# The stretch between the two layers of a graph network kernel: another order of SyncE's transfers, edge ends in pairs, count checks inside the second product, and conversions taken from GpSimd

## The reference

```python
h = jnp.maximum(_layernorm(x), 0.0)                       # layer 0
ea = edge_attr @ W_edge.T + b_edge
msg = relu(h[src] + ea)
aggr = segment_sum(msg, dst, num_segments=N_NODES)
u = relu(((1.0 + eps) * h + aggr) @ W1.T + b1)
x = x + u @ W2.T + b2                                     # "second product" = u @ W2.T

h = jnp.maximum(_layernorm(x), 0.0)                       # layer 1
m = relu(h[src]) + EPS
ex = exp(m - segment_max(m, dst)[dst])
msg = segment_sum(ex / segment_sum(ex, dst)[dst] * m, dst)
x = x + (h + msg) @ W + b
```

## Time and profile before

| | us |
|---|---|
| time, median of 3 runs | 2461.71 |
| lowest, highest | 2456.18, 2465.78 |
| the profiled execution's own time | 2460.79 |
| its span (what the trace covers) | 2459.0 |
| layer 0 and its end (trace, to about) | 2026 |
| two products, layer norm, `table16` and its transfers (to about) | 2120 |
| layer 1 (from the third block on) | 339 |

### The profile page before, as it was taken

The page is one execution under the profiler, slowest core; times in us unless marked ns, Lnnn a source line. Parts: engine busy times, 40 slices in busy tenths (PEclk is TensorE's granted clock), DMA queues, the critical chain, the costliest instruction groups (busy, mean ns, idle before and its releaser), DMA issues.

```text
span 2459.0 us, 54222 instructions
## 1 busy us (share of the span) xinstructions
PE 1809.7 (74%) x11221; PEld 1497.2 (61%) x11222; DVE 1908.5 (78%) x4568; ACT 760.4 (31%) x1320; POOL 1767.9 (72%) x1801
## 2 busy tenths in 40 slices
PE   3677776767766776766766767776767767699999
PEld 2466665655555565655655556655655655588887
DVE  9999997878778887878787878777887878354454
ACT  5001121222233333344444444444544555000000
POOL 4777777777777777777777777777777762477774
PEclk9899888888888888888888888887888896899999
DMA  5234344444444444444444455454554533877774
GB/s 162 48 83 105 95 108 106 108 105 113 115 107 127 122 118 120 122 130 125 129 126 127 133 129 136 135 139 126 149 134 128 145 111 133 292 270 259 263 273 151
DMA packets 172680, 344.69 MB, mean 140 GB/s; under 512 B 72897, under 2 KB 126971, under 8 KB 158286
## 3 DMA queue, kind: packets, MB, share of 16 engines
q1 hardware_dynamic: 33586, 153.14, 21.2%
q0 software_dynamic: 60864, 99.55, 17.9%
q10 hardware_dynamic: 77990, 89.82, 10.7%
HBM read 247.65 MB, written 94.68 MB: 139 GB/s over the span
## 4 chain that ended last, share of the span: by engine, by line
POOL 59%; issue 19%; PE 15%; DVE 2%; DMA 2%; SPq 2%; ACT 1%; POOLq 0%; ACTq 0%; DVEq 0%
POOL rows_buf L585 59%; PE ps L849 11%; PE ps L859 2%; DMA rows_buf<-table,index 1%; PE ps L680 1%; SPq L531 1%; SPq L545 1%; ACT features_buf L932 0%; DVE zone L1364 0%; PE ps L826 0%; PE ps L872 0%; PE ps L772 0%; DVE ps L1327 0%; SPq L537 0%; PE ps L670 0%
## 5 line engine op out<-in xcount | busy, mean ns | idle before, releaser
L585 POOL DMA_INDIRECT rows_buf<-table,index x1539 | 1511.6, 982 | 496.5 <-issue 493.2
L772 PE MATMUL ps<-zone,planes 128*128 128x400 f16 x2352 | 620.5, 379 | 555.9 <-DVE zone L1364 467.1
L1364 DVE TENSOR_SCALAR zone<-iota_c,planes 128x400 f16<-128x400 int16 x2352 | 678.1, 341 | 60.9 <-issue 50.9
L990 ACT ACTIVATE features_buf<-ps 128x800 f16<-128x800 f32 x392 | 327.8, 836 | 1240.2 <-PE ps L772 1233.7
L772 PEld LDWEIGHTS ps<-zone,planes 128*128 128x128 f16 x2352 | 251.3, 107 | 733.6 <-issue 675.7
L670 PEld LDWEIGHTS ps<-wet,zone 128*128 128x128 f32 x3136 | 551.0, 250 | 35.3 <-issue 30.5
L670 PE MATMUL ps<-wet,zone 128*128 128x96 f32 x3136 | 535.7, 330 | 0.0
L657 PE MATMUL ps<-onehot,features_buf 128*96 128x128 f32 x3120 | 428.4, 283 | 0.0
L657 PEld LDWEIGHTS ps<-onehot,features_buf 128*96 128x96 f32 x3120 | 395.1, 174 | 12.0 <-issue 1.3
L1327 DVE TENSOR_TENSOR ps<-ps,rows_buf 128x768 f32<-128x768 f32 x171 | 164.6, 963 | 256.1 <-DMA rows_buf<-table,index 235.5
L1125 DVE TENSOR_TENSOR planes<-ps,planes 128x1536 f16<-128x1536 f32 x196 | 341.3, 1741 | 0.0
(11 more groups left out here) (186 smaller groups left out, 811.0 us busy)
## 6 DMA issues: line engine op xcount, KB each, us to landing
counts<-features_buf ACTq DMA_DIRECT2D x392, 200.0 KB
zone<-edge_t SPq DMA_DIRECT2D x98, 768.0 KB
single<-table SPq DMA_DIRECT2D x3072, 0.4 KB
rows_buf<-counts SPq DMA_DIRECT2D x24, 1600.0 KB, 6.8
rows_buf<-table,index POOLq DMA_INDIRECT x1539
planes<-counts SPq DMA_DIRECT2D x12, 1600.0 KB
weighted<-planes SPq DMA_DIRECT2D x5, 840.0 KB
final<-residual ACTq DMA_DIRECT2D x48, 48.0 KB
```

Of the source, the lines that this page charges most:

```text
L585: nc.gpsimd.indirect_dma_start(out=into[:, t, :], out_offset=None, in_=table, in_offset=bass.IndirectOffsetOnAxis(ap=at[:, t:t + 1], axis= ...
L772: nc.tensor.matmul(count_ps[:, bass.ds(banks[k], WC)], row_hot[:, u % 2, g * GS + k, :], pair_hot[:, g * GS + k, :], start=False, stop=Fal ...
L990: nc.scalar.activation(count_out[:, k], bank, ACT.Copy, accum_out=row_sum[:, bass.ds(p, 1)]).then_inc(moved, 1)
L1364: last = nc.vector.tensor_scalar(pair_hot[:, k, :], iota_c[:, :], step_pair[:, bass.ds(i * (IS * SC) + (u * SC + k), 1)], None, ALU.is_equal)
```

## The change

Five things change, all between the layers.

1. **Order on SP.** The waits and stores are put in another order (the rows below). The counts of block 1 still wait for `node_out`; those of block 2 come after the fifth unit's own rows. A unit's store of the four parts (`weighted_store`) stands among the stores of own rows (`own_store`). The two loads of `own` stand before the last `weighted_store`.
2. **Edge ends in pairs.** `edge_src` and `edge_dst` are one input `edge_ends[2, ...]`, and a fetched block's sources and destinations come in one transfer of twice as many rows: 13 transfers instead of 26.
3. **Count checks.** The three small PE instructions stand after the first of the ten groups of the second product, the matmul for `block_start` after the fourth, and DVE copies `block_start` in the loop after the second unit's moments.
4. **No GpSimd conversions.** The high part of exp(h) is made by DVE for units 0, 1 and 3, and by ACT for units 2 and 4. GpSimd only gathers.
5. **HBM tensors.** `hidden` and `weighted` are gone; own rows go to `table0`, the four parts to `table1` seen as float16 (same shapes and sizes). ACT reads its copy of the flag inside the loop instead of ahead of it.

```diff
@@ sp @@
+                def own_store(u):
                     sp.wait_ge(features, NU + u + 1)
                     for part in (slice(0, EVEN), slice(EVEN, NP)):
-                        sp.dma_start(hidden.rearrange("(p j) d -> p j d", j=NJ)[part, units[u], :],
+                        sp.dma_start(own_rows.rearrange("(p j) d -> p j d", j=NJ)[part, units[u], :],
                                      hs[part, units[u], :]).then_inc(own_out, 16)
...
+                block_load(0)
+                sp.wait_ge(starts_ready, 1)
+                for g, start in enumerate(load(sp, block_start, DB, GB, [E] * GB)):
+                    n = FETCH[g]
+                    sp.dma_start(fetch_ends[:, :, FETCH_AT[g]:FETCH_AT[g] + n],
+                                 edge_ends[:, bass.ds(start, P * n)].rearrange("e (p k) -> p e k", k=n)
+                                 ).then_inc(fetch_in, 16)
+                sp.wait_ge(node_out, NG)
+                block_load(1)
...
+                for u in range(NU - 2):
+                    own_store(u)
+                weighted_store(0)
+                weighted_store(1)
+                own_store(NU - 2)
+                weighted_store(2)
+                own_store(NU - 1)
+                block_load(2)
+                weighted_store(3)
                 sp.wait_ge(own_out, 2 * NU * 16)
                 sp.wait_ge(step_done, SC + NSTEP)
                 for b in range(2):
-                    sp.dma_start(own[:, b, :], hidden[b * P:(b + 1) * P, :]).then_inc(residual_in[b], 16)
+                    sp.dma_start(own[:, b, :], own_rows[b * P:(b + 1) * P, :]).then_inc(residual_in[b], 16)
+                weighted_store(4)
@@ pe @@
+            def count_checks(g):
+                if g == 0:
+                    pe.wait_ge(bad_ready, 3)
+                    nc.tensor.transpose(ps[0:1, 6, 0:P], bad[:, 2:3], ident[:, :])
...
+                if g == 3:
+                    pe.wait_ge(edges_moved, 1)
+                    nc.tensor.matmul(ps[0:1, 5, 0:NB], block_edges[:, :], upper[0:NB, 0:NB], start=True, stop=True
+                                     ).then_inc(starts_ps, 1)
...
                     last.then_inc(node_ps, 1)
+                    if layer == 0:
+                        count_checks(g)
@@ act @@
                 exp_of(3)
+                exp_high_of(2)
                 product_high(2)
                 feature(1, NU - 1)
                 exp_of(4)
+                exp_high_of(4)
@@ dve @@
                 moments_of(1, u)
+                if u == 1:
+                    dve.wait_ge(starts_ps, 1)
+                    nc.vector.tensor_copy(block_start[:, :], ps[0:1, 5, 0:NB]).then_inc(starts_ready, 1)
```

More of the change, by code:

```diff
@@ L80 @@
 NE = 4
+HIGH_ON_ACT = (2, 4)
 NW2 = 2
@@ L1627 @@
     dst_tiles = tiles(dst, QT * P, NPAD)
[L1628 to L1630 removed]
+    ends = np.zeros((2, E + EPAD), np.int32)
+    ends[1] = NPAD
+    ends[0, :E] = np.asarray(src)
+    ends[1, :E] = np.asarray(dst)
     arrays = {
```

90 lines of the change are left out of this document (38 added, 52 removed).

## The result

The changed kernel takes **2429.1 us** (median, 2425.8 to 2431.2) where the kernel before takes 2460.3 (2456.2 to 2465.8) beside it: a ratio of 0.987 (95% interval 0.985 to 0.989). The forecast of 2448.9 us and its range from 2445 to 2455 are both missed; the gain is 31 us and not 12.8. The profiled execution has a span of 2424.0 us against 2459.0 before, 35.0 us less.

A forecast was written before the change was run, and what follows sets the result against it. It took SP's queue between the layers to delay layer 1, which runs at PE's pace. Gathers gain 10.0 us (8.7 + 0.9 + 0.4), plus 2.8 spare: 12.8 off the median 2461.7 gives 2448.9 us, range 2445 to 2455.

The forecast's parts named there:

- 59% of it is GpSimd's gathers of layer 0, which the change leaves alone: Layer 0: its gathers are 59% of the chain and keep their time; only what lies behind them is at stake.
- I cost the whole conversion item at nothing: Between the layers: moving GpSimd's five conversions gains 0 us, being covered by transfers; 3 us cost if the cover were gone.
- The prediction's own test: Layer 0: the forecast is wrong if its 2026 us move by more than 1 us.
- Edge ends ahead of `node_out`: SP's queue: 13 pairs from 2058.6 at 0.52 us each take 6.8 us, ending at 2065.4, ahead of 2066.8.
- The slower rival: SP's queue: a paired transfer takes longer than two did; slower from 1.6 us each, 2468.4 us at 2.1; chance 0.03.
- The hole closes: SP's queue: legs of 16.2 and 28.5 us join without the 8.7 us hole, saving 0.9 us start-up; gathers 9.6 us earlier.
- Conversions on DVE and ACT: Between the layers: DVE gets three, ACT two, about 1.0 us each, against GpSimd's 3042 ns for each of five.
- Count checks: Second product: ten matmul rows run in PE's 2.13 us wait; gain 0.4 us on `node_out`, ends 0 and 1.3.
- `own` ahead of the last parts: SP's queue: `own` lands 10.0 + 3.0 = 13.0 us earlier, at 2106.5; PE's 20.0 us wait shrinks to 7 to 9.
- the rival in which `own` comes no earlier than the parts: Start of layer 1: `own` lands no earlier than the parts, PE and gathers both gain 10.0 us: 2451.7 us; chance 0.10.
- What is late next: Layer 1, second fetched block: gathers start 10.0 us earlier with 2.8 us spare, allowing a gain of 12.8 us.
- the rival of the gathers behind a block's counts: Layer 1: gathers queue behind 1600 KB of counts, up to 4.6 us late; gain 8.2, 2453.5 us; chance 0.12.

The follow-up runs named there:

- e4: Kernel before, masked, with SyncE's new order and moved count checks alone, two transfers for each block's edge ends: 2455.5 us, ratio 0.996.
- c0: Kernel before, with the wait values that ACT and PE load from memory masked to 16 bits: 2462.1 us, ratio 1.002.
- the control: Changed kernel with masked wait values and no other edit, run on the same chip as the early loads of `final`: 2428.7 us, ratio 0.986.
- e1: Kernel before, masked, with own rows in `table0` and the four parts in `table1`, no other edit: 2457.4 us, ratio 0.999.
- e2: Kernel before, masked, with the five conversions moved from GpSimd to DVE (three) and ACT (two), no other edit: 2442.8 us, ratio 0.993.
- e3: Kernel before, masked, with the edge ends in 13 transfers of pairs in the old place, no other edit: 2451.6 us, ratio 0.997.
- f5: Changed kernel, masked, with ACT issuing the loads of `final` for the first four blocks ahead of its wait for own rows: 2434.4 us, ratio 0.988.

## Why the prediction was wrong, by its own steps

**"59% of it is GpSimd's gathers of layer 0, which the change leaves alone."** This is the step that failed, together with **"I cost the whole conversion item at nothing"**. The price was looked for where the conversions stand, and there it is nothing: the seam takes 52.7 us instead of 53.1 without them, and 42.5 instead of 41.8 with them, both within its spread. But GpSimd's instructions between the layers set the price of all its gathers, and 1539 of them in a chain turn 11 ns into 17 us. It is nearly the whole distance of 20 us between forecast and result. Why the gathers take that price is open (see above); that it comes with the conversions is shown from both sides. The prediction's own test, that layer 0's 2026 us must not move by more than 1 us, is what caught it. The seam alone would have given some 12 us, and 2449 us. The profiled pair of executions flatters the change by some 4 us more, which are TensorE's clock (an estimate: 3.0 us in the first product and 0.9 behind it, by the numbers under the count checks).

**Edge ends ahead of `node_out`: right.** 0.52 us for a pair was chosen between 0.52 and 1.04, and 0.53 measured (6.92 / 13). They ended at 2042.1, 1.0 us before SP went past `node_out` (1.4 forecast). `e4` shows the other end: 1.0 us for two, 4.0 us late. The slower rival needed 1.6 us for a pair. The rule quoted with it (the Trainium skill, "DMA: Bandwidth & Descriptors", section "Why a DMA increments its semaphore by 16 and not by 1"), sixteen DMA engines where 128 is outermost, agrees with the trace. SP's queue shows these packets for the 13 transfers, from 2035.2 to 2043.5:

```profile
q1 hardware_dynamic: 3536, 0.25, 31.9%
```

That is 13 x 272. The rows of ends are 13 x 256, and the other 208, of 4 bytes each, are 16 for a transfer.

**The hole closes: right but for 0.9 us.** The two legs, 16.2 and 28.5 us, sum to 44.7, and from the counts of block 1 (2043.15) to the first gather (2087.89) it takes 44.7 us. The hole of 8.7 us is gone to a tenth. The 0.9 us taken for one start of an empty queue less did not appear.

**Conversions on DVE and ACT: right in the seam.** DVE's took less than the 1.0 us assumed, ACT's as much (line, busy us, mean ns):

```profile
L1042 ACT ACTIVATE planes<-zone 125x960 f16<-125x960 f32 x2 | 2.0, 996 | 0.0
L1492 DVE TENSOR_SCALAR planes<-zone 125x960 f16<-125x960 f32 x3 | 2.0, 654 | 0.0
```

**Count checks: right in kind, 0.4 us forecast and some 0.9 found.** The table above doesn't show this, because the clock moves its rows. Ahead of the second product PE stood for 2.7 us behind the first (2.1 of waiting, then the three small instructions) in all five kernels with the old place of the checks, and 1.3 us in all fifteen with the new one. In these 1.3 us it waits for the first product's results on DVE, so the product begins 1.4 us sooner and not the whole 2.7:

```profile
2023.06 1.33 PE L700 MATMUL ps<-w2s,rows_buf 96*125 96x96 f32 x10 [1.30 <-DVE rows_buf L1452]
```

Half a microsecond of the 1.4 comes back inside the product. From the end of the first product to the last addition, `c0` and `e4`, at the same granted clock:

```profile
2044.37:2068.36 23.99, 21.43 (x108) 20.79 (x107) 20.19 (x108) 9.91 (x28) 0.00 (x0) 0.57 0.19 70
2042.92:2066.01 23.09, 21.11 (x107) 20.22 (x107) 20.18 (x109) 9.90 (x28) 0.00 (x0) 0.57 0.28 80
```

It is 0.9 us less with the checks moved, inside the prediction's ends of 0 and 1.3. The clock takes the rest of the 4.2 us: it lies between two levels here (0.50 is 1.2 GHz, 1.00 is 2.4). It was 0.61 on average from 2028 to 2036 in the kernel before, in the first product, and 1.00 in the same place of the changed one; the whole first product took 16.2 and 13.2 us. From its end to the last addition it was 0.59 and 0.85, in 23.2 and 21.4 us, of which 0.9 are the checks. The control had 0.79 and 14.5 us:

```profile
2028.00:2036.00 8.00, 8.00 (x26) 5.26 (x25) 6.06 (x12) 2.54 (x5) 0.00 (x0) 0.61 0.08 28
```

```profile
2009.00:2017.00 8.00, 7.85 (x31) 5.35 (x32) 6.36 (x14) 3.43 (x6) 0.00 (x0) 0.79 0.08 28
```

The first of these rows is of the kernel before, the second of the control. This isn't the change's doing: `e1`, `e2` and `e3`, which have neither the new order nor the moved checks, ran their first product in 13.1 us at 1.00.

**`own` ahead of the last parts: right mechanism, some 1.3 us too much.** PE's turn came 11.3 us earlier behind `node_out` where 12.6 (13.0 without the checks' 0.4) were forecast: 0.9 is the start-up that didn't appear, 0.2 the 2.8 us by which PE gained on the gathers instead of 3.0, and the last 0.2 is not accounted for. PE gained more than the gathers did (11.3 and 8.6 us), so the rival in which `own` comes no earlier than the parts fell. PE's wait is 10.5 us, not 7 to 9, because PE's work ahead of it ended 31.2 us behind `node_out` (2084.90 - 10.54 - 2043.12) instead of 33.1. Whether `final` or `own` lands last changes nothing, as `f5` shows.

**What is late next: right.** The gathers start 3.0 us behind PE's turn, where it was 0.2, and layer 1 takes 339.1 us as before. The only wait of PE behind its first turn is one of 2.1 us, which the kernel before has too:

```profile
PE ps L881 <- DVE soft L1570: 2.1, 1, 2.1
```

So the rival of the gathers behind a block's counts fell. The rule that spoke against it (the Trainium skill, "DMA: Bandwidth & Descriptors", section "Queues, rings and completion order": queues take turns packet by packet) fits the trace, which shows no wait there; no run shows the turns themselves.

## What to carry to other kernels

What else runs on an engine that issues one instruction 1500 times in a chain can change the price of that instruction: before costing an edit on that engine at nothing because it is off the path, multiply a change of one per cent in that instruction by its count, and keep that in the range. Put small transfers where the queue is empty: the same 13 took 6.9 us there and 15.6 behind 5.6 MB, 9.4 of them in two at which SP was stopped, so read such a group transfer by transfer and not by its mean. When two small loads are issued together into a full queue, advancing one alone gave nothing here. Before reading a stretch of a few microseconds between two traces, see whether both had the same granted clock in it.

## What was not expected of the hardware

- A gather of GpSimd takes 955 or 944 ns over a whole execution, and three or five tensor_scalars executed between the layers, behind the last gather of layer 0 (57 to 2036 us later in the kernel before), decide it, even of 128x1 and 0.2 us each. One doesn't, five ahead of the first gather don't, five that aren't run don't.
- GpSimd's fourth instruction, a memset, takes 0.10 us in kernels that execute a tensor_scalar on GpSimd later, and 0.12 to 0.13 us in those that execute none.
- Single gathers of 6.3 to 8.9 us appear in some executions. In `f5` the longest is 5.8 us longer than in its control, and the last gather of layer 0 comes 7.3 us later.
- A transfer of two lists of 15 to 20 columns on 128 partitions holds SP for 0.37 to 0.41 us (one is begun every 0.54 us), and as long behind 5.6 MB in the queue, but for two of 13, at which SP was stopped for 8.2 and 1.2 us.
